# A graph attention layer: the first index list in two parts, more gathers without a question, earlier counts and attentions

## What is computed

```python
feats = (X @ W).reshape(-1, H, D)
a_self, a_neigh = einsum(feats, att_self), einsum(feats, att_neigh)      # per node and head
scores = leaky_relu(a_self[i] + a_neigh[j], 0.2)                         # only where A[i, j] is 1
attn = softmax(scores over j)
out = relu(attn @ feats + bias)
x = layernorm(x + out)
```

## Time and profile before

| | |
|---|---|
| median of 3 runs | 821.96 us |
| the profiled execution, device time | 821.55 us |
| its span, first to last instruction | 819.7 us |
| granted TensorE clock, mean | 0.788 |
| TensorE matmul, busy | 586.2 us (72%) |
| VectorE busy | 604.7 us (74%) |
| GpSimd busy | 505.3 us (62%) |
| ScalarE busy | 78.3 us (10%) |
| moved by DMA | 291.76 MB, mean 356 GB/s |
| chain that ended last | DMA 44%, PE 31%, DVE 17%, issue 5%, POOL 2% |

### The profile page before, as it was taken

One profiled execution on the slowest core, in us unless ns is written; L12 is line 12 of the kernel. 1 busy time (PEld: TensorE's weight loads), 2 busy tenths in 40 slices (PEclk: granted clock), 3 DMA queues, 4 the chain that ended last, 5 costly groups with the idle time before them and its releaser, 6 DMA issues.

```text
span 819.7 us, 8741 instructions
## 1 busy us (share of the span) xinstructions
PE 586.2 (72%) x2094; PEld 293.3 (36%) x2133; DVE 604.7 (74%) x1748; ACT 78.3 (10%) x355; POOL 505.3 (62%) x463
## 2 busy tenths in 40 slices
PE   2965656687769787786969776877987968783454
PEld 1711111144414344342515342543533423351333
DVE  7466997561895896867677758599887689779875
ACT  1200000120010101010010100101111010120010
POOL 1000787777727777777777777778581757575700
PEclk9966655669689979695969785978968777996778
DMA  7999999999999999999999999999999999991200
GB/s 282 361 421 363 410 397 396 397 398 398 397 411 402 392 399 401 398 399 397 398 400 397 398 398 375 333 397 399 407 397 411 407 398 406 399 393 28 50 1 26
DMA packets 67974, 291.76 MB, mean 356 GB/s; under 512 B 23062, under 2 KB 31051, under 8 KB 35152
## 3 DMA queue, kind: packets, MB, share of 16 engines
q1 hardware_dynamic: 48528, 275.40, 84.9%
q0 software_dynamic: 14208, 10.46, 4.4%
q10 hardware_dynamic: 5184, 5.31, 1.9%
HBM read 294.36 MB, written 4.75 MB: 365 GB/s over the span
## 4 chain that ended last, share of the span: by engine, by line
DMA 44%; PE 31%; DVE 17%; issue 5%; POOL 2%; ACT 0%; POOLq 0%; SPq 0%; another core or an unknown queue 0%; DVEq 0%; ACTq 0%
DMA adj_sb<-in_adj_dram 44%; PE xt_ps L666 15%; PE codes L638 11%; DVE spare L922 3%; PE ft_ps L707 2%; POOL near L434 2%; DVE near L760 1%; PE xt_ps L668 1%; PE ft_ps L623 1%; DVE val L807 1%; DVE top L908 1%; DVE z L899 1%; DVE key L868 1%; DVE z L907 1%; DVE left L870 1%
## 5 line engine op out<-in xcount | busy, mean ns | idle before, releaser
L434 POOL DMA_INDIRECT near<-node_table,idx x444 | 502.1, 1131 | 275.3 <-issue 214.4
L638 PE MATMUL codes<-adj_sb,weights 128*128 128x512 bf16 x992 | 327.3, 466 | 156.8 <-DMA adj_sb<-in_adj_dram 153.5
L638 PEld LDWEIGHTS codes<-adj_sb,weights 128*128 128x128 bf16 x1024 | 99.9, 107 | 364.2 <-issue 301.0
L666 PE MATMUL xt_ps<-spare,ident 128*128 128x360 f32 (+4 forms) x734 | 203.0, 426 | 34.7 <-DVE spare L922 34.6
L666 PEld LDWEIGHTS xt_ps<-spare,ident 128*128 128x128 f32 x734 | 139.0, 203 | 90.9 <-issue 51.7
L807 DVE MAX8 val<-codes 128x8 f32<-128x128 f32 x192 | 42.8, 285 | 110.3 <-PE codes L638 97.7
L922 DVE TENSOR_TENSOR spare<-near,spare 128x704 f32<-128x704 f32 (+12 forms) x64 | 101.3, 1644 | 7.1 <-ACT spare L561 7.1
L812 DVE MAX8 val<-codes 128x8 f32<-128x64 f32 (+2 forms) x156 | 19.6, 201 | 30.3 <-PE codes L638 29.6
L561 ACT ACTIVATE spare<-z 128x736 f32<-128x736 f32 (+10 forms) x16 | 14.9, 933 | 229.5 <-DVEq L914 229.5
L868 DVE MAX8 key<-left 128x8 f32<-128x168 f32 (+2 forms) x79 | 28.5, 361 | 2.2
L631 PE MATMUL codes<-place,weights 128*128 128x512 bf16 x58 | 28.7, 495 | 0.3 <-issue 0.2
(11 more groups left out here) (160 smaller groups left out, 475.7 us busy)
## 6 DMA issues: line engine op xcount, KB each, us to landing
adj_sb<-in_adj_dram SPq DMA_DIRECT2D x256, 1024.0 KB, 16.9
near<-node_table,idx POOLq DMA_INDIRECT x444
node_table<-spare ACTq DMA_DIRECT2D x4, 648.0 KB, 9.7
spare<-in_x_dram SPq DMA_DIRECT2D x4, 512.0 KB, 7.4
self_sb<-node_table ACTq DMA_DIRECT2D x16, 121.5 KB, 7.5
x_sb<-in_x_dram SPq DMA_DIRECT2D x4, 384.0 KB, 18.3
out_dram<-x_sb SPq DMA_DIRECT2D x1, 768.0 KB, 15.9
self_sb<-node_table ACTq DMA_DIRECT2D x16, 40.5 KB, 10.0
```

Source lines behind the costliest of these rows:

```text
L434: pool.indirect_dma_start(out=near[:, near_at(t) + k, :], out_offset=None, in_=table[:, :], in_offset=bass.IndirectOffsetOnAxis(ap=idx[t % ...
L638: last = pe.matmul(codes[i][:, :], weights[:, kk, :], adj_bf[q][:, k * GC:(k + 1) * GC, 1], start=False, stop=(kk == BITS - 1))
L666: last = pe.matmul(to[:, a:b, :], ident[:, :], slot_rows(t, s, a, b), start=(s == 0), stop=(s == W - 1))
```

## The change

- `ATTEND` gets other steps: turns 1 to 10 one step sooner each, 11 to 14 two steps, 15 one. Sums and finishings move along with it, by the rule above: the sum of turn 0 from step 20 to 19, of turn 5 from 39 to 38, of turn 10 from 55 to 53, of turns 11 to 15 from 59, 62, 65, 68, 71 to 57, 60, 63, 66, 70.
- `FIRST` gets larger: 366 slots in all become 442, so fewer are asked for.
- The counts of turns 10 to 14 are made in step 4(t + 1) + 1 instead of + 2.
- In turn 0 the first 32 slots of the list are handed over after four of the ten rounds, with a signal of their own; GpSimd starts on them and waits for the rest at slot 32.

```diff
-    ATTEND = [16, 20, 24, 28, 32, 36, 39, 42, 45, 48, 51, 55, 58, 61, 64, 67]
+    ATTEND = [16, 19, 23, 27, 31, 35, 38, 41, 44, 47, 50, 53, 56, 59, 62, 66]
-    FIRST = [54, 33, 28, 25, 24, 22, 21, 20, 19, 19, 18, 18, 17, 16, 16, 16]
+    FIRST = [60, 38, 34, 31, 30, 28, 26, 24, 23, 22, 22, 22, 21, 21, 20, 20]
+    HEAD_SLOTS = 32
+    def count_at(t):
+        return RING * (t + 1) + (2 if t < 10 else 1)
...
             def gather(t):
                 S, first = SLOTS[t], FIRST[t]
-                wait_apart(pool, idx_ready, t + 1)
+                if t > 0:
+                    wait_apart(pool, idx_ready, t + 1)
...
                 for k in range(first):
+                    if t == 0 and k == 0:
+                        wait_apart(pool, idx_begun, 1)
+                    if t == 0 and k == HEAD_SLOTS:
+                        wait_apart(pool, idx_ready, 1)
                     slot(k)
...
-                if i == 2 and t:
+                if t and n == count_at(t - 1):
                     count_slots(t - 1)
...
-                if i == 2 and t:
+                if t and n == count_at(t - 1):
                     count_keys(t - 1)
...
                     step(dve.max(key[:, t % KEY_RING, o], src[:, 0:C]))
                     if r < S // 8 - 1:
                         step(dve.match_replace(rest_keys[:, 0:C], key[:, t % KEY_RING, o], src[:, 0:C], 0.0))
-                step(dve.tensor_copy(key_i[:, 0:S], key[:, t % KEY_RING, 0:S]))
+                    if t == 0 and 8 * r + 8 == HEAD_SLOTS:
+                        step(dve.tensor_copy(key_i[:, 0:HEAD_SLOTS], key[:, 0, 0:HEAD_SLOTS]))
+                        dve.tensor_scalar(idx[0][:, 0:HEAD_SLOTS], key_i[:, 0:HEAD_SLOTS].bitcast(u32), ROW - 1, None, ALU.bitwise_and).then_inc(idx_begun, 1)
+                d = HEAD_SLOTS if t == 0 else 0
+                step(dve.tensor_copy(key_i[:, d:S], key[:, t % KEY_RING, d:S]))
...
-                dve.tensor_scalar(idx[t % IDX_RING][:, 0:S], key_i[:, 0:S].bitcast(u32), ROW - 1, None, ALU.bitwise_and).then_inc(idx_ready, 1)
+                dve.tensor_scalar(idx[t % IDX_RING][:, d:S], key_i[:, d:S].bitcast(u32), ROW - 1, None, ALU.bitwise_and).then_inc(idx_ready, 1)
```

More of the change, by code:

```diff
@@ L291, in gat_resnorm @@
         count_ready = sem("count_ready")
+        idx_begun = sem("idx_begun")
         idx_ready = sem("idx_ready")
```

## The result

The changed kernel takes 865.58 us (median of 4 runs, 863.93 to 868.33) against 822.77 us of before on the same chip: a ratio of 1.053 [1.0501, 1.0559]. Slower, as forecast, but by 43 us instead of 29, and above the range of 838 to 861. The profiled execution has a span of 862.5 us (819.7 before).

The account below looks back on a forecast made before the run. The adjacency stream was taken to bound the kernel up to about 741 us, then a fixed chain behind the last list. List 15 at 784 against 752.4, less 1.6, made +29.7: 851 us, range 838 to 861.

Parts of the forecast that it names:

- First list, `FIRST`, counts: Turn 0's split list, extra unasked slots, earlier key counts: gathering starts at 80.7 instead of 85.8 us, nothing gained or lost overall.
- the 6 us held against them: VectorE's last six rounds of turn 0's list: gathers beside them could delay them up to some 6 us, by the port-lock rule.
- Middle: Turns 1 to 5 and 9 attend in list steps, so weighing comes 10 us later: +8 us, bounds −5 and +16.
- the early turns are some 5 us longer, a wait that seven quarters in flight cover: Sums of turns 1 to 4, a step more: waits some 5 us longer than turn 10's, hidden by the stream's buffers.
- the places of turns 0, 5 and 9: Three sums where TensorE waits for late weighing, against one before: 3 × 4.6 − 4.6 = 9 us later.
- turn 10 of before: Evidence for cover: weighed by 643.8, summed from 644.87, 1.1 us to spare, stream at 407 GB/s.
- The price of 4.6 us per place: Stream lost per late sum, from turn 6 of before: 353 against 398 GB/s from 492 to 533 us.
- The upper bound of +16: Highest loss allowed for the early attentions of turns 1 to 5 and 9, where +8 us was taken.
- Rival 2: Each of turns 1 to 9 loses 4.6 us of stream, 37 instead of 8, about 880 us; chance 10%.
- List 13 to list 14: GpSimd start 1.0, 23 gathers with stretching 32.5, VectorE resuming 1.6, attending 6.4, peeling and list 10.3: 51.8 us.
- The 1.6: Time from the end of a turn's last gather until VectorE goes on (781.3 to 783.0): 1.6 us.
- List 14 to list 15, and the end: Gathers, attending, exponentials, weighing, peeling and list: 54.7 us, list 15 at 784; same chain behind it, 1.6 us shorter.

Follow-up runs that it names:

- short sums with the same waits: Kernel before with turn 1's attention in step 19 instead of 20 and every second matmul of the sums of turns 0 and 1 left out: 821.65 us, 0.9989.

## Why the prediction was wrong in size and right in kind

**First list, `FIRST`, counts: right.** First gather at 78.67 (80.7 forecast), hole ahead of turn 2 16.6 us (16), 455 gathers, TensorE's wait at the keys of turn 14 8.3 us (7), time unchanged when only these edits stand. The last six rounds of the first list, now beside gathers, still take 0.35 us each, so the 6 us held against them didn't come. One thing of the counts was missed: where a list is late, TensorE waits at the count, and ahead of a sum this adds to the wait there (2.7 us at the count of turn 11, then 5.1 at the sum of turn 9).

**Middle: wrong, +8 where it is 22 (844.3 us, 1.0269 of before; the holes of the changed kernel's trace give 19.5 more than before).** The step that failed is "the early turns are some 5 us longer, a wait that seven quarters in flight cover". The waits came about as long as that: 7.2 us in turn 1, 4.8, 4.1 and 2.8 in turns 2 to 4. In turns 3 and 4 the cover held (398 to 401 GB/s), in turns 1 and 2 it didn't (313 and 371 GB/s, 4.6 and 1.5 us of stream), and the places of turns 0, 5 and 9 lost 18 us instead of 13.8. In the same step the sum's other pieces take up to 6 us per quarter, so buffers aren't given back in time; short sums with the same waits lost nothing. What was taken for evidence, turn 10 of before, had no wait and a shorter sum. Its quarters, from TensorE's timeline of the kernel before:

```profile
644.87 1.40 PE L666 MATMUL xt_ps<-spare,ident 128*128 128x360 f32 x2
...
649.22 1.06 PE L638 MATMUL codes<-adj_sb,weights 128*128 128x512 bf16 x4
...
653.15 1.06 PE L638 MATMUL codes<-adj_sb,weights 128*128 128x512 bf16 x4
...
656.00 1.07 PE L638 MATMUL codes<-adj_sb,weights 128*128 128x512 bf16 x4
```

Three pieces take 11.1 us there (644.87 to 656.00); turn 0's take 19.8 after (243.67 to 263.5), time for seven quarters of the stream, while three are taken.

Nor is the cover one number. These two sums, the first of before (turn 7), the second of after (turn 6), wait as long as those that lost, with a rate of 393 to 399 GB/s beside them:

```profile
538.11 1.54 PE L666 MATMUL xt_ps<-spare,ident 128*128 128x360 f32 x2 [5.00 <-DVE spare L922]
...
509.67 1.54 PE L678 MATMUL xt_ps<-spare,ident 128*128 128x360 f32 x2 [6.66 <-DVE spare L938]
```

Both come soon behind a hole, where the sixteen parts of a load land 1 to 2.4 us apart instead of up to 8.5; that this is why is argued, not tested.

The price of 4.6 us per place was wrong too, and it was taken from a hole that cost no time. Turn 0's place alone costs 9: turn 1, attended in a list step, is weighed late as well and its sum waits, and the piece behind a wait runs at the lower clock at first. Turn 5's place costs 8.7 us of stream, with a wait of 12.7 us. Turn 9's cost 2. The upper bound of +16 was built from the same price, so the range fell with it. Rival 2, each of the turns 1 to 9 paying 4.6, was nearer for turns 1 and 2; turns 3, 4, 6, 7 and 8 paid nothing, and at 37 us it was too dear.

**List 13 to list 14: 55.6 us, forecast 51.8.** The 23 gathers take 33.6 us from first start to last end (32.5 allowed), and VectorE goes on 4.9 us behind the last one's end (722.04 + 1.00 to 727.95), not 1.6: this is the second step that failed. The 1.6 was taken from turn 15, where no stream runs; beside it turn 14 of this kernel gives 1.4 (773.49 to 774.86), also with hardly any stream. The waits that followed were 6.75 us for turn 13 (0 to 5 forecast) and 14.0 for turn 14 (16).

**List 14 to list 15, and the end: right.** 53.5 us (54.7) and 65.0 from list 15 to the end of the span, against 67.3 in before (−2.3; −1.6 forecast). The last sum begins at the low clock as before. Halving turn 14's gathers and moving the list ahead of the attention each gave back what this account says.

The miss adds up: 11.4 + 3.8 − 1.2 − 0.7 = 13.3 us, and 862.5 + 1.85 − 851.2 = 13.2.

## What to carry to other kernels

Seven buffers in flight are not seven buffers of cover: first take off what the same engine does between the quarters in that very step, and how far apart the parts of a load land, then set the wait against the rest, with the lower clock behind the wait added. Read the price of a stall from when the last parts land, not from a dip in GB/s. When a late product makes an engine wait, moving one consumer only shows the next one (sum, then count): go through everything that the engine reads from the late one in that step. And a gain in the stream's middle has to be followed to the last list before it is counted.

## What the runs showed of the hardware

- A gather's landing beside the stream. The last gather of turn 13 is landed for VectorE 5.9 us after its start (722.04 to 727.95), with the stream at 400 GB/s; the last of turn 14 2.4 us (772.49 to 774.86), with the stream over. With ten slots gathered in turn 14, the row of turn 13 was the same (5.8 us behind the last start, beside the stream), and turn 14's last gather, at 763.60 with some 116 GB/s of other traffic, took 3.7. The Trainium skill (DMA: Bandwidth & Descriptors, section on the anatomy of one DMA) gives a fixed cost of about 2.0 us, most of it the receipt of the last write; the row without the stream agrees, the one beside it is 3.5 us longer. That the stream is the cause was not tested by itself.
- Behind the wait of 4.7 us on TensorE the granted clock is 0.67 over the next 8.3 us, where the same 16 matmuls ran at 1.00. It was at 0.50 before the wait began, so the wait can't be called its only cause.
- The sixteen parts of a 1 MB load drift apart while the stream runs without a break (in before 3.4 us apart at step 19, 8.5 at step 42) and come together when it stalls (1.3 at step 45). A dip in the rate with the parts apart delayed the last ones by nothing; the changed kernel's middle, where the last parts did come late, cost time.
- The two slow gathers of the first turn (8.34 us at 85.37) met other slots than in the earlier trace rows, but again beside VectorE's 8192-column operations: a SCALAR_TENSOR_TENSOR of 8.67 us runs from 84.18 to 92.85, and the gather ends 0.86 us behind it. The Trainium skill (SBUF — State Buffer, section on the two separate sides) tells of a port pair locked for a whole instruction; the rows agree. The earlier head, the two needless gathers of turn 1 and these stalls vanish in the 16.6 us hole; the other nine needless ones in GpSimd's wait ahead of turn 12, 12.53 us with the attentions put back, 18.70 in before.
